# A fused layer on eight cores: longer TensorE warm-up bursts, and GpSimd's two operations per output tile in the other order

## What is computed

```
xn = layernorm(x)                                  # x: 2 x 4096 x 4096
q, k, v = split(conv1d(xn, conv_w, width 3), 3)    # 4096 -> 3 x 1024
qh, kh, vh = q @ wq, k @ wk, v @ wv                # 16 heads of 64
p = softmax(mask(qh @ kh.T / 8)) in blocks of 128 tokens
s = (p @ vh) @ wo @ proj_w                         # back to 4096
sc = softmax(xn @ router_weight.T)                 # 64 experts
w_sum, w_dense = sum and scatter of the 8 largest of sc
g = silu(xn * w_sum + w_dense @ expert_bias)
out = x + s * g
```

## Time and profile before

| what | value |
|---|---|
| timed runs (two) | 1883.42 and 1979.96 us, median 1931.69 |
| the profiled execution's own time | 1875.22 us |
| its span on the slowest core (core 2) | 1873.7 us |
| spans of the eight cores | 1862.8 to 1873.7 us |
| mean granted TensorE clock by core | 0.859 to 0.866 |
| TensorE matmuls busy | 1556.8 us, 83% of the span |
| VectorE, ScalarE, GpSimd busy | 393.8, 383.5 and 229.3 us |
| convolution | about 210 to 1190 us of the span |
| output stage | about 1588 to 1873.7 us |

### The profile page before, as it was taken

One profiled execution on the slowest core, in us unless ns is written; L12 is line 12 of the kernel. 1 busy time (PEld: TensorE's weight loads), 2 busy tenths in 40 slices (PEclk: granted clock), 3 DMA queues, 4 the chain that ended last, 5 costly groups with the idle time before them and its releaser, 6 DMA issues.

```text
span 1873.7 us, 18861 instructions; the slowest of 8 cores (1862.8 to 1873.7 us)
## 1 busy us (share of the span) xinstructions
PE 1556.8 (83%) x7874; PEld 759.1 (41%) x7996; DVE 393.8 (21%) x644; ACT 383.5 (20%) x453; POOL 229.3 (12%) x180
## 2 busy tenths in 40 slices
PE   4455799999999999999999999988567656788682
PEld 4355444444444444444444444433344334222220
DVE  2877200000000000000000000000642551256465
ACT  1443000000000000000000000098543542232332
POOL 0000111111111111111111111000000000125244
PEclk8677899999999999999999999999555555788776
DMA  6999566666666666666666666642100006422424
GB/s 141 212 241 181 69 77 79 74 74 78 79 73 74 78 79 72 75 79 79 72 75 79 77 72 76 90 79 50 41 1 1 1 14 120 104 90 106 164 90 179
DMA packets 230825, 163.68 MB, mean 87 GB/s; under 512 B 74691, under 2 KB 222403, under 8 KB 226499
## 3 DMA queue, kind: packets, MB, share of 16 engines
q0 software_dynamic: 155472, 92.97, 39.3%
q1 hardware_dynamic: 75270, 69.50, 13.6%
HBM read 220.69 MB, written 16.78 MB: 127 GB/s over the span
## 4 chain that ended last, share of the span: by engine, by line
PE 58%; DMA 11%; DVE 8%; ACT 6%; another core or an unknown queue 5%; POOL 4%; SPq 4%; issue 3%; POOLq 0%; DVEq 0%; ACTq 0%
PE pCv L650 53%; DMA AL<-x 6%; DMA AL<-pw 4%; SPq L432 2%; POOL AL L1067 2%; ACT AL L712 2%; POOL AL L1070 2%; DVE AL L805 1%; PE pQ L734 1%; SPq L437 1%; DVE tRs L797 1%; ACT L712 1%; DVE tStat L326 1%; DVE tSc L783 1%
## 5 line engine op out<-in xcount | busy, mean ns | idle before, releaser
L650 PE MATMUL pCv<-AL 128*128 128x512 bf16 x4515 | 995.5, 379 | 5.0
L650 PEld LDWEIGHTS pCv<-AL 128*128 128x128 bf16 x4608 | 449.6, 98 | 550.6
L783 DVE TENSOR_REDUCE tSc<-pS 128x1 f32<-128x512 f32 x32 | 21.9, 684 | 1191.0 <-PE pS L776 1104.6
L593 POOL DMA_DIRECT2D AL<-cw x144 | 125.9, 875 | 1055.1 <-PE pCv L650 862.2
L665 ACT ACTIVATE AL<-pCv,tCbT 128x512 bf16<-128x512 f32 x48 | 29.0, 687 | 889.2 <-PE pCv L650 889.2
L470 PE MATMUL pLgT<-AL 128*64 128x128 bf16 x768 | 59.9, 256 | 90.2 <-DMA AL<-AL 90.2
L999 PE MATMUL pPr<-AL 128*128 128x512 bf16 x436 | 117.5, 413 | 13.8 <-DVE AL L1047 13.1
L931 PE MATMUL pWO<-AL 64*128 64x256 bf16 x512 | 109.8, 414 | 5.7 <-DVE AL L857 5.7
L470 PEld LDWEIGHTS pLgT<-AL 128*64 128x64 bf16 x768 | 58.8, 136 | 91.3 <-issue 91.3
L931 PEld LDWEIGHTS pWO<-AL 64*128 64x128 bf16 x512 | 73.2, 144 | 41.4 <-issue 6.6
L817 PE MATMUL pPT<-tI,AL 128*128 128x128 bf16 x128 | 18.7, 300 | 75.6 <-DVE AL L805 75.6
(11 more groups left out here) (97 smaller groups left out, 915.7 us busy)
## 6 DMA issues: line engine op xcount, KB each, us to landing
AL<-cw POOLq DMA_DIRECT2D x144, 512.0 KB, 5.9
AL<-x SPq DMA_DIRECT2D x16, 2048.0 KB, 11.9
out<-AL SPq DMA_DIRECT2D x8, 2048.0 KB, 7.4
AL<-pw POOLq DMA_DIRECT2D x8, 1024.0 KB, 8.2
AL<-wq POOLq DMA_DIRECT2D x1, 2048.0 KB, 19.4
AL<-wk POOLq DMA_DIRECT2D x1, 2048.0 KB, 17.5
AL<-wv POOLq DMA_DIRECT2D x1, 2048.0 KB, 15.6
AL<-wo POOLq DMA_DIRECT2D x1, 2048.0 KB, 17.1
```

The costliest lines, as they stand in the source:

```text
L593: sCWs[gi % 4].add(e.dma_start(out=cwr[:, gi % 4, :].rearrange("p (g f) -> p g f", g=8), in_=d_cw[s, g].rearrange("g p f -> p g f")), 16)
L650: ins = e.matmul(p_cv[:, 512 * (bs + 2 * sub + hf): 512 * (bs + 2 * sub + hf) + 512], lhsT, xnTh[:, o:o + 512], start=(step == 0), stop=(s ...
L783: cNM.add(e.reduce_max(nmax[Q % 2][:], p_S[:, 512 * (Q % 2):512 * (Q % 2) + 512], axis=AX.X, negate=True), 1)
```

## The change

It does two independent things. First, the warm-up bursts get longer: 600 for 290 at the start, 128 for 32 after each of the routing tiles 0 to 6, 16 for 8 after tile 7, and 200 for 50 ahead of the convolution. Second, in stage 4 GpSimd's two operations change places: the add of the tile before now stands ahead of the multiply of this tile. For this, GpSimd's multiplies count in a semaphore of their own, cLO, and cPL counts VectorE's alone, so that where VectorE waited for cPL at 2tt it now waits for cPL at tt and cLO at tt. The new GpSimd add waits for cLO, that is for GpSimd's own multiply of that tile. Lines behind L1038 have other numbers in the new kernel (L1042 is L1043, L1047 is L1048, L1052 is L1054, L1077 is L1080, GpSimd's multiply L1067 is L1074, its add stays L1070; L1099 is L1103, L1106 is L1110).

```diff
-            warm(e, 290)
+            warm(e, 600)
...
-                    warm(e, 8 if j == NTILE - 1 else 32)
+                    warm(e, 16 if j == NTILE - 1 else 128)
...
-                warm(e, 50)
+                warm(e, 200)
...
                     if tt >= 1:
-                        e.wait_ge(cPL.h, 2 * tt)
+                        e.wait_ge(cPL.h, tt)
+                        e.wait_ge(cLO.h, tt)
                     e.wait_ge(sX6[tt % 2].h, 16 * (tt // 2 + 1))
...
                     if tt >= 1:
-                        e.wait_ge(cPL.h, 2 * tt)
+                        e.wait_ge(cPL.h, tt)
+                        e.wait_ge(cLO.h, tt)
                         cFIN.add(e.tensor_add(s6[(tt - 1) % 2][:, 1536:4096],
...
                 @GP
                 def _(e, tt=tt):
-                    e.wait_ge(cSIL.h, 2 * tt + 1)
-                    cPL.add(e.tensor_mul(s6[tt % 2][:, 0:1536], s6[tt % 2][:, 0:1536],
-                                         gw[:, 0:1536]), 1)
                     if tt >= 1:
+                        e.wait_ge(cLO.h, tt)
                         cPLe.add(e.tensor_add(s6[(tt - 1) % 2][:, 0:1536],
                                               s6[(tt - 1) % 2][:, 0:1536],
                                               x6[(tt - 1) % 2][:, 0:1536]), 1)
+                    e.wait_ge(cSIL.h, 2 * tt + 1)
+                    cLO.add(e.tensor_mul(s6[tt % 2][:, 0:1536], s6[tt % 2][:, 0:1536],
+                                         gw[:, 0:1536]), 1)
...
             @DV
             def _(e):
-                e.wait_ge(cPL.h, 16)
+                e.wait_ge(cPL.h, 8)
+                e.wait_ge(cLO.h, 8)
                 cFIN.add(e.tensor_add(s6[7 % 2][:, 1536:4096],
...
             @GP
             def _(e):
-                e.wait_ge(cPL.h, 16)
+                e.wait_ge(cLO.h, 8)
                 cPLe.add(e.tensor_add(s6[7 % 2][:, 0:1536], s6[7 % 2][:, 0:1536],
```

## The result

| | before | changed kernel |
|---|---|---|
| median of all timed runs | 1894.05 us (10 runs) | 1844.8 us (11 runs) |
| the profiled execution's own time | 1875.22 us | 1849.95 us |
| span of its slowest core | 1873.7 us (core 2) | 1848.4 us (core 3) |
| spans of its eight cores | 1862.8 to 1873.7 us | 1816.8 to 1848.4 us |

The ratio is 0.9752 with a 95% interval of 0.972 to 0.9784: 2.5% faster. The ratio leaves out executions of either kernel in which the cores of a die took longer at a lower granted clock, such as the 1979.96 us that made the median of the first two runs 1931.7. The sum of the prediction was a gain of 50.2 us, or 2.7% of the profiled 1875.2, and its forecast of 1829 us lay between two bases; measured is a gain of 2.5%. The cores now lie 32 us apart in one execution, where it was 11, and that spread is what the forecast missed.

A forecast was written before the change was run, and what follows sets the result against it. The bound was taken to be a loop of waits in the last stage, with GpSimd's late add holding store and load. +8.3 - 55.3 - 3.2 = -50.2 us gave 1825.0 or 1833.2; forecast 1829 us, midway, range 1812 to 1845.

The forecast's parts named there:

- The release of the store: Stage 4: VectorE's high add, not GpSimd's late low add, releases store and load; 9.2 us less per period, 55.3 in all.
- The period of 23.4 us: Stage 4 loop: each period falls from 32.6 to 23.4 us, with the load's landing of 12.6 us unchanged.
- Rival B: Stage 4: loads get slower as store and load fill 12.6 of 23.4 us; 11 us lost, 1840 us; chance 0.10.
- TensorE as what is late next, at 21.8 us: Stage 4: TensorE needs 21.8 us per tile against 23.4, so the load remains the bound by 1.6 us.
- The store of the s6 buffer: Stage 4: the store freeing s6 lands by 20 us of the period, so ScalarE's evictions no longer hold the bias matmuls.
- The added wait on cLO and the tail: Stage 4: VectorE's added wait costs 0, at most 1.4 us; after the last gate, one GpSimd add fewer gains 3.2 us.
- The last burst: Ahead of the convolution: 150 more warm-ups cost 8.3 us on the path and buy nothing.
- The other bursts: At the start and around the routing tiles: longer warm-ups are hidden, taken as 0, between -0.2 and +1.4 us.
- Rival A: Stage 4 shared port: GpSimd's multiply goes before VectorE's high add; period 26.8 us, 20 us lost, 1849 us; chance 0.10.
- C: Stage 4: the reorder doesn't act, something else of equal age holds the store; 1888 us; chance 0.04.
- D: Convolution: runs at a lower clock, slower than before; at 0.90 it costs 109 us, giving 1938 us; chance 0.06.
- The base: Time the gain is taken from: profiled 1875.2 us gives 1825.0, lower timed run 1883.4 gives 1833.2; forecast midway.

## Why the prediction was right, and where it was off

- **The release of the store.** Right: SyncE waits for VectorE's high add, and the 9.2 us for GpSimd's are gone.
- **The period of 23.4 us.** Right as a mechanism, mis-sized. "Everything from SyncE on stays as it is" is the step that failed. The 12.6 us of landing which it took from the period of before is not a property of the load: 11.7 us with the neighbour out of step (period 22.45 on core 5, 1671.85 to 1694.30), 15.2 in step (25.6 to 26.3). The slowest core sets the time, and in five of the eight profiles of the table at least one of the four pairs is less than 4 us apart over the whole loop or nearly so.
- **Rival B.** Its size was about right (11 us; it cost 13.6 on core 3), its cause wrong: the share of time that the transfers fill doesn't do it, the distance to the neighbour's does, in the old order too.
- **TensorE as what is late next, at 21.8 us.** The order of the bounds was right; the figure was 20.75, since tile 1's row held a piece at half clock. In the run with the high add early the clock stays at 1.00 and the smaller figure holds.
- **The store of the s6 buffer.** Right that it is covered with the store first; the exchanged order showed by how little.
- **The added wait on cLO and the tail.** Right: from the gate to the high add it is 7.38 to 7.46 us in the changed kernel, against 7.36, so 0.1 us a period at most; and the tail gave 3.3 us against 3.2.
- **The last burst.** Right: 8.4 us from the starts of the convolution, 10 to 11 in the medians. The other bursts: 0 was forecast, 1.4 found. Tile 7's matmuls do follow the burst with no gap, but the copy of halo rows doesn't hide all of that: VectorE's wait behind it grew by 1.1 us on average. "They buy nothing" is true of the 150 more and not of the first 50, without which three cores started the convolution at half clock.
- **Rival A** didn't come: VectorE kept its 0.09 us. **C** is out by the waits. **D** is out: the clock over the convolution is 1.00 on every core of all fourteen profiles.
- **The base.** The gain in percent was right to 0.2; the time in us was 16 too low, because the profiled run of before had no pair in step, while most of its runs are 1885 to 1898. The slow landings, which the sum leaves out, come in both kernels and so nearly cancel in the gain. That was luck.
- **The range.** The 1844.8 us lie at the upper end of 1812 to 1845. The terms given for that end add up to 1833.2 + 1.4 + 1.4 + 7.1 = 1843.1, not 1845, and none of them but the 1.4 for tile 7 came; what filled the place was the slow loads. That the time falls inside is luck too.

## What to carry to other kernels

An operation that frees a buffer belongs right behind the one that makes its input, on each engine that has a share of it; freeing it early on one of two moved the bound by 9 us a tile, and on both took the transfer off the path and was worth 4.5 to 4.9% in all (ratios 0.9549 and 0.9514). Ask which transfer, load or store, is waited for last before exchanging them. What a burst of warm-ups has beyond the point where the clock is up on every core costs its whole length: 150 more cost 8.4 us here, while leaving out the last 50 gained nothing that can be told, since three cores then began at half clock. And a transfer's landing read from one profile holds for that phase of the neighbour core only: look at all eight cores, and take the slowest pair's figure when the time is the slowest core's.

## What was unexpected of the hardware

A store and a load of 2 MB each, issued back to back, land in 11.9 us (median, from the load's issue to the gate; 11.7 to 14.3) when the other core of the pair is more than 6 us away with its own, and in 15.0 to 16.6 us when they are less than 2 us apart (table above); a load of the same size on another pair of the die at that moment leaves the median at 11.9. Issued second, the load takes 11.8 and the store 7 to 9; issued first, the load takes 9.6 and the store 14.1 on core 0. With no burst ahead of it, TensorE started the convolution at full clock on five cores, on core 4 behind 16 small matmuls at half clock and a gap of 1.3 us, and at half clock on the other three, for 3.4 to 4.8 us.
